# Position products of a two-layer attention kernel: all twelve heads at once, in one stage

## The reference

```python
# layer 0: attention over all 1024 positions, with relative positions
rel_h = jnp.einsum('bhwc,hkc->bhwk', r_q, Rh)
rel_w = jnp.einsum('bhwc,wkc->bhwk', r_q, Rw)
attn_bias = (rel_h[:, :, :, :, None] + rel_w[:, :, :, None, :]).reshape(Bx * NUM_HEADS, S, S)
scores = q @ jnp.swapaxes(k, -1, -2) * SCALE + attn_bias
out = softmax(scores) @ v
# layer 1: 7 x 7 neighbourhood attention plus 16 register tokens
scores = jnp.where(mask_cat[None, None], q @ k_cat.T * scale, NEG_INF)
```

## Time and profile before

| | |
|---|---|
| median of 3 runs | 4896.54 us (4892.41 to 4898.04) |
| the profiled execution | 4902.5 us, span 4900.8 us |
| TensorE matmul busy | 4491.2 us, 92% of the span |
| VectorE busy | 3079.3 us, 63% |
| ScalarE busy | 2608.5 us, 53% |
| POOL busy | 892.5 us, 18% |
| mean granted clock of TensorE | 0.951 |

### The profile page before, as it was taken

The page is one execution under the profiler, slowest core; times in us unless marked ns, Lnnn a source line. Parts: engine busy times, 40 slices in busy tenths (PEclk is TensorE's granted clock), DMA queues, the critical chain, the costliest instruction groups (busy, mean ns, idle before and its releaser), DMA issues.

```text
span 4900.8 us, 97559 instructions
## 1 busy us (share of the span) xinstructions
PE 4491.2 (92%) x32598; PEld 2291.5 (47%) x32598; DVE 3079.3 (63%) x5558; ACT 2608.5 (53%) x3955; POOL 892.5 (18%) x1901
## 2 busy tenths in 40 slices
PE   5879999999999999999999999999999999999998
PEld 3334453544535454453544535455454544535444
DVE  3736667665675656667566675656657566676654
ACT  1533556555564555556555564555646555565564
POOL 3112111222202212121212202212021121102111
PEclk7888999999999999999999999999999999999999
DMA  6334242443414433253433424433144432424401
GB/s 126 83 73 86 49 104 62 99 90 70 89 39 106 87 87 71 53 108 70 99 79 70 88 52 99 94 73 84 44 106 81 99 79 48 101 62 99 87 14 40
DMA packets 235869, 386.05 MB, mean 79 GB/s; under 512 B 58396, under 2 KB 133728, under 8 KB 235360
## 3 DMA queue, kind: packets, MB, share of 16 engines
q1 hardware_dynamic: 189280, 266.13, 23.8%
q10 hardware_dynamic: 21504, 75.51, 7.6%
q0 software_dynamic: 24576, 37.80, 4.8%
HBM read 227.79 MB, written 88.08 MB: 64 GB/s over the span
## 4 chain that ended last, share of the span: by engine, by line
PE 75%; DVE 9%; SPq 5%; issue 5%; DMA 5%; ACT 2%; DVEq 0%; ACTq 0%; POOL 0%
PE P L1135 15%; PE P L1153 14%; PE P L1094 13%; PE P L958 6%; PE P L959 6%; DVE mx L901 5%; PE P L1071 5%; PE P L1185 4%; PE P L1206 4%; PE P L1102 3%; DMA QA<-queries 2%; PE P L1178 1%; SPq L507 1%; DMA biases<-xn 1%; DVE mxc L907 1%
## 5 line engine op out<-in xcount | busy, mean ns | idle before, releaser
L901 DVE TENSOR_REDUCE mx<-P 128x1 f32<-128x512 f32 x3072 | 1923.2, 682 | 471.2 <-PE P L1094 467.9
L771 ACT ACTIVATE probs<-P 128x1024 f32<-128x1024 f32 x1536 | 1507.5, 1022 | 777.7 <-PE P L1153 777.0
L1094 PE MATMUL P<-K,AR 96*128 96x256 f16 x6144 | 1093.1, 282 | 42.9 <-DMA AR<-biases 26.7
L1153 PE MATMUL P<-AR,K 113*128 113x512 f16 x3072 | 924.8, 383 | 14.1 <-DMA AR<-mrow 13.6
L907 DVE TENSOR_REDUCE mxc<-P 128x1 f32<-128x336 f32 (+1 forms) x1536 | 648.2, 474 | 307.6 <-PE P L1103 304.0
L787 ACT ACTIVATE probs<-P 128x320 f32<-128x320 f32 (+3 forms) x1632 | 618.1, 436 | 405.2 <-PE P L1206 340.0
L1135 PE MATMUL P<-probs,V 128*17 128x512 f32 x6144 | 817.2, 604 | 9.9 <-ACT probs L771 9.9
L1094 PEld LDWEIGHTS P<-K,AR 96*128 96x128 f16 x6144 | 541.7, 99 | 566.9 <-DVE mx L901 198.3
L1153 PEld LDWEIGHTS P<-AR,K 113*128 113x128 f16 x3072 | 216.9, 98 | 676.6 <-ACT probs L771 517.8
L1206 PE MATMUL P<-A,K 113*128 113x320 f16 (+2 forms) x1536 | 447.1, 306 | 12.9 <-ACT probs L787 12.1
L1102 PE MATMUL P<-K,A 112*128 112x320 f16 (+1 forms) x1536 | 400.4, 295 | 53.4 <-DVE mx L901 35.8
(11 more groups left out here) (122 smaller groups left out, 3705.4 us busy)
## 6 DMA issues: line engine op xcount, KB each, us to landing
AR<-biases SPq DMA_DIRECT2D x384, 256.0 KB, 7.7
AR<-queries ACTq DMA_DIRECT2D x96, 512.0 KB, 5.8
biases<-xn SPq DMA_DIRECT2D x192, 256.0 KB, 2.9
AR<-queries ACTq DMA_DIRECT2D x96, 256.0 KB, 8.5
K<-oraw POOLq DMA_DIRECT2D x384, 64.0 KB, 4.8
xin<-in_x_dram SPq DMA_DIRECT2D x16, 768.0 KB, 10.5
queries<-oraw SPq DMA_DIRECT2D x384, 32.0 KB, 4.8
QA<-queries SPq DMA_DIRECT2D x192, 64.0 KB, 5.1
```

The lines of the kernel that those rows point to most:

```text
L771: nc.scalar.activation(probs[:, u % RING, j:j + 2, :], P[:, b:b + 2, :], ACT.Exp).then_inc(p_done[0], 1)
L901: V_.reduce_max(mx[:, n // 2, n % 2:n % 2 + 1], bank, AX.X).then_inc(used, 1)
L1094: last = mm(bank[:, QD * (v % 2):QD * (v % 2) + QD], AR[0:ROWS_MAX[0], part % SLOTS, v, c, j, 128 * q:128 * q + 128], K0[0:ROWS_MAX[0], h, ...
L1153: last = mm(P[:, j, :], K0[0:ROWS, h, 128 * kt:128 * kt + 128], AR[0:ROWS, p % SLOTS, kt // 2, :, j, :], start=True, stop=True)
```

## The change

The products of all 12 heads of image i+1 run in main1, in 16 jobs at steps 6 to 26 (`rel_jobs(image)`, `RELS = 16`). A job handles 2 lines, 2 matmuls each, of 192 columns, so a table's loaded operand serves all heads; `n // 8` is the table, and a bank holds 384 columns. QA holds all three groups and the first job waits for all of them. `relhi` and `rello` of the first table lie in `oraw`, those of the second in `xn` and in `xin`; ScalarE waits (`rel_moved`) for `biases_out` before its next output copy. Biases leave by table (2 x 3 stores), and the slots fill by table: at step 19 and at step 28. SP's `operands_out` now also issues the loads of QA of groups 1 and 2, that of group 1 ahead of group 2's stores, that of group 2 at the end. The first 22 maxima jobs of phase 1 stay in main1, the other 11 move to main0; the first 18 of local group 2 move from main1 to the main0 before it. POOL's row of ones is set once an image. `rcp` lies in QA's space.

```diff
-RELS = 4
+RELS = 16
+SECOND, THIRD = 22, 18
...
-    return {"rel": 4, "stat": 1, "max": (7, 5)[job[1]]}[job[0]]
+    return {"rel": 6, "stat": 1, "max": (7, 5)[job[1]]}[job[0]]
...
     else:
-        placed = evenly(max_jobs(0, image, 2), 0, 20)
+        placed = evenly(max_jobs(0, image, 1)[SECOND:], 0, 6) + evenly(max_jobs(0, image, 2), 6, 23)
...
-    placed += [(8 + n, job) for n, job in enumerate(rel_jobs(image, 2))]
...
-        placed += evenly(max_jobs(1, i1, 0), 13, 32) + evenly(max_jobs(1, i1, 1), 77, 94)
+        placed += evenly(max_jobs(1, i1, 0), 15, 34) + evenly(max_jobs(1, i1, 1), 75, 87)
+        placed += evenly(max_jobs(1, i1, 2)[:THIRD], 87, 95)
...
-    placed = evenly(max_jobs(1, image, 2), 0, 25)
-    placed += [(2 + n, job) for n, job in enumerate(rel_jobs(n0, 0))]
-    placed += [(0, ask(n0, 0)), (5, fill(n0, 0)), (6, ask(n0, 1)), (6, fill(n0, 1))]
-    placed += [(24 + n, job) for n, job in enumerate(rel_jobs(n0, 1))]
-    placed += [(28, ask(n0, 2)), (28, fill(n0, 2))]
-    placed += evenly(max_jobs(0, n0, 0) + max_jobs(0, n0, 1), 25, STEPS[1] - TAIL)
+    third = max_jobs(1, image, 2)[THIRD:]
...
+    rel = rel_jobs(n0)
+    placed = evenly(third[:8], 0, 6) + evenly(third[8:], 28, 38)
+    placed += evenly(rel, 6, 27) + [(0, ask(n0, 0)), (6, ask(n0, 1)), (28, ask(n0, 2))]
+    placed += [(19, fill(n0, p, 0)) for p in range(SLOTS)] + [(28, fill(n0, p, 1)) for p in range(SLOTS)]
+    placed += evenly(max_jobs(0, n0, 0) + max_jobs(0, n0, 1)[:SECOND], 39, STEPS[1] - TAIL)
...
+        QA = sb("QA", [128, G, GH, QD], F16)
+        staged = (flat[:, 0:G * S // 2], xn[:].rearrange("p a n -> p (a n)")[:, 0:G * S // 2])
+        relhi = [t.bitcast(F16).rearrange("p (m q) -> p m q", q=QD) for t in staged]
+        staged = (flat[:, G * S // 2:G * S], xin[:].rearrange("p t c -> p (t c)"))
+        rello = [t.bitcast(F16).rearrange("p (m q) -> p m q", q=QD) for t in staged]
...
-            def biases_away(im, g):
+            def biases_away(im, table):
...
-                    sp.wait_ge(ready, (im * G + g + 1) * RELS)
-                    for table in range(2):
+                    sp.wait_ge(ready, im * RELS + 8 * table + 8)
+                    for g in range(G):
...
-                    if g == 1:
-                        query_blocks(im, 0)
+                    if g:
+                        query_blocks(im, g - 1)
...
+                query_blocks(im, G - 1)
...
+            def rel_moved():
+
+                while staged_rel:
+                    image = staged_rel.pop()
+                    for table in range(2):
+                        act.wait_ge(biases_out[table], (image + 1) * PER_BIASES)
...
             def local_out(im, g, half):
 
                 rows_moved()
+                rel_moved()
...
-                    for b in range(8):
-                        line = 8 * (n % 2) + b
+                    for g in range(G if n == 0 else 0):
+                        pe.wait_ge(qa_in[g], (image + 1) * PER_QA)
+                    q = QA[:].rearrange("p g h (l w) -> p (g h) l w", w=16)
+                    table = n // 8
+                    for b in range(2):
+                        line = 2 * (n % 8) + b
                         rhs = q[:, :, :, line] if table else q[:, :, line, :]
                         for s in range(2):
                             lhs = Z[:, table, s, 15 - line:47 - line, :].rearrange("p x a -> p (x a)")
-                            last = mm(bank[:, 64 * b:64 * b + 64], lhs, rhs, start=(s == 0), stop=(s == 1))
+                            last = mm(bank[:, 16 * NH * b:16 * NH * b + 16 * NH], lhs, rhs,
+                                      start=(s == 0), stop=(s == 1))
```

More of the change, by code:

```diff
@@ L77, in max_jobs, with rel_jobs @@
     return [("max", layer, image, part, n) for n in range(ITEMS[layer] + 1)]
-def rel_jobs(image, g):
-    return [("rel", 0, image, g, n) for n in range(RELS)]
+def rel_jobs(image):
+    return [("rel", 0, image, 0, n) for n in range(RELS)]
 def stat_jobs(layer, image):
@@ L90, with fill, fills @@
 MOVES = ("fill", "ask")
-def fill(image, phase):
-    return "fill", 0, image, phase, 0
+def fill(image, phase, table):
+    return "fill", 0, image, phase, table
+def fills(image, phases):
+    return [fill(image, phase, table) for phase in phases for table in range(2)]
 def ask(image, phase):
@@ L198, in block_stages @@
     else:
-        yield "jobs", 0, n0, first_phases(n0, *max_jobs(0, n0, 1), *stat_jobs(1, i0))
+        yield "jobs", 0, n0, first_phases(n0, *max_jobs(0, n0, 1)[:0 if is_image(n0, 0) else SECOND], *stat_jobs(1, i0))
 def before_loop():
@@ L379, in consumed @@
             if kind == "rel":
-                return rello_done, (image * G + part) * RELS + n + 1
+                return rello_done, image * RELS + n + 1
             if kind == "stat":
@@ L486, in fill_slot @@
                     sp.wait_ge(st_done[0], im * STEPS[0] + (p - SLOTS + 1) * STEPS[0] // PHASES[0])
[L487 to L495, removed]
+                for b in range(2):
+                    rows_ = biases[g, table, D * b:D * b + D, :, 2 * half:2 * half + 2, :, :]
+                    rows_ = rows_.rearrange("k s a h n -> (k s) (a h n)")
+                    same = slice(2 * b, 2 * b + 2) if table == 0 else slice(b, VAR, 2)
+                    sp.dma_start(AR[32 * table:32 * table + 32, p % SLOTS, same, :, :, :],
+                                 rows_.unsqueeze(1).broadcast_to((32, 2, 2 * GH * QD))).then_inc(ar_in[p], 16)
@@ L514, in moves @@
                 if what == "fill":
-                    fill_slot(image, part)
-                    if part in (0, 2):
-                        query_blocks(image, part // 2 + 1)
-                    if part == 1 and is_image(image, 0):
+                    fill_slot(image, part, n)
+                    if part == SLOTS - 1 and n and is_image(image, 0):
                         static_rows()
-                if what == "rel" and n == RELS - 1:
-                    biases_away(image, part)
+                if what == "rel" and n % 8 == 7:
+                    biases_away(image, n // 8)
                 if what == "max" and n == ITEMS[layer]:
@@ L565, in stage @@
                         sp.wait_ge(mid_out, stored)
+                        if not (isinstance(im, int) and im + 2 >= B):
+                            sp.wait_ge(biases_out[1], (im + 3) * PER_BIASES)
                         sp.dma_start(xin[:], mid[im]).then_inc(mid_in, 16)
@@ L697, in stage @@
                 again = kind == "jobs" and any(job[0] == "rel" for e in after for _, job, _ in e)
-                if again or kind == "out" and (L == 0 or not (isinstance(im, int) and im + 2 >= B)):
-                    g, image = (1, im) if again else (2, im) if L == 0 else (1, im + 2)
-                    pool.wait_ge(biases_out[g], (image + 1) * PER_BIASES)
+                if again or kind == "out" and L == 1 and not (isinstance(im, int) and im + 2 >= B):
+                    image = im if again else im + 2
+                    pool.wait_ge(biases_out[1], (image + 1) * PER_BIASES)
                     take_wait()
-                    done, count = (ones_again, im + 1) if again else (ones_done[L], im + 1)
+                    done, count = (ones_again if again else ones_done), im + 1
                     nc.gpsimd.memset(xn[CH:CH + 1, 1, :], 1.0).then_inc(done, 1)
@@ L807, in high_parts @@
                     if job[0] == "rel":
+                        if job[4] == 0:
+                            rows_moved()
+                            staged_rel.append(job[2])
                         act.wait_ge(rel_done, consumed(job)[1])
@@ L1225, in deliver @@
                     last.then_inc(ot_done[L], 1)
-                if L == 0 or not (isinstance(im, int) and im + 2 >= B):
-                    pe.wait_ge(ones_done[L], im + 1)
+                if L == 1 and not (isinstance(im, int) and im + 2 >= B):
+                    pe.wait_ge(ones_done, im + 1)
                 for q in range(2):
```

56 lines of the change are left out of this document (27 added, 29 removed).

## The result

The changed kernel takes 5281.23 us (median of 4 runs, 5275.71 to 5288.34) against 4895.58 us before (4 runs): the ratio is 1.079, 95% interval 1.077 to 1.081. It is slower by 386 us. 258 us were forecast, with a range up to 5260, so the time lies just outside it. The profiled execution took 5277.37 us with a span of 5275.1, 374.3 us above that of before; the forecast for that difference was 257.

A forecast was written before the change was run, and what follows sets the result against it. TensorE, 75% of the span, was taken as the bound, with every wait ahead of it. Main1 +19.2 us and main0 -2.3 made +16.9 a turn, +237 over 14 turns, +257 with the ends: 5154 us, range 4950 to 5260.

The forecast's parts named there:

- The queries are needed earlier: Main1, step 6: TensorE waits for all three groups' queries, idle 17 us, going on at about +20.5.
- Steps 6 to 27: Main1 stretch holding the position products: 30 us, bounds 24 and 35, so step 28 begins at +50.5.
- price by the column: Second-table products in main1: every strided column costs 2.0 ns, so they still take 12.3 us.
- The new wait on ScalarE: Main1, behind step 29: first output copy waits for the biases; TensorE loses 6 us, bounds 0 and 8.
- about enough: Main1: second-table fills have ten steps until the maxima of phase 0 at step 39; no wait priced.
- Main1 as a whole: Sum of main1's terms: 101.5 us against 82.3, +19.2 a turn.
- Net -2.3 us: Main0: products leaving save 7.8 us, maxima jobs moved in add 5.5 with bank waits.
- covered while TensorE has more: Main0: VectorE's extra work of about 11 us on 111 of 151 was expected to cost no time.
- If the jobs no longer interleave so well, it is 0: Main0's unfavourable case: no net saving in place of -2.3 us.
- Ahead of the loop: Images 0 and 1 before the loop: later queries, more products and fills ahead of the maxima, +25 us together.
- The rivals: Main1: queries come in time, 4873 or 4790 us, chance 0.09; or little changes, 4895 us, chance 0.05.
- stride by matmul: Second-table products in main1: stride paid per matmul, 5.4 us in place of 12.3, total about 5000 us; chance 0.10.

The follow-up runs named there:

- ninth run: Changed kernel, query rows of slots 0 and 1 asked for at step 6 and of slot 2 at step 45 of main1: 5173.0 us.
- sixth run: Changed kernel, second table's products read adjacent columns as the first table's do (horizontal products left wrong): 5248.1 us.
- fourth run: Changed kernel, ScalarE's output copies wait for the biases of the first table alone: 5276.5 us.
- tenth: Changed kernel, 18 maxima jobs of local group 2 back in main1, 33 of local group 1 at main0 steps 77 to 94: 5226.0 us.
- thirteenth run: Changed kernel, moved maxima of phase 1 and local group 2 back in main1, local group 1's at main0 steps 77 to 94: 5253.9 us.

## Why the prediction was right in direction and too small

*The queries are needed earlier.* Right in mechanism and size. TensorE reached step 6 at +4.0 (forecast +3.5) and went on at +20.6 (+20.5). The ninth run shows the part of slot 0's fill, 4 us. The prediction did not say that fresh queries are not the only condition: without their wait, 6.6 us of waiting for ScalarE's copy space remain.

*Steps 6 to 27.* 25.3 us against a forecast of 30, near its lower bound: the first-table part went faster than taken, step 16 at +28.5. The second-table part took 17.4 us, forecast 20. The price by the column holds: a matmul of 192 columns takes 0.39 us (1.57 us for four), where a price by the matmul would have made 0.17. Four take 1.55 us at a granted clock of 1.00 (at 1624.57) and 1.57 at 0.50 (at 1630.62), and the sixth run with adjacent columns takes 7.0 us for the stretch. This agrees with the Trainium skill (SBUF — State Buffer, the note on cachelines): every strided column costs.

*The clock.* Main1 has 0.77 of its clock where it had 0.88. It falls twice ahead of step 28. The first fall, at 1604.0, lies within the long wait and lasts until 1621.1, in the first-table products. This agrees with the rule of the Trainium skill (TensorE: Matmul & The Clock Gate, Why this matters for your kernels) that spoke against the change. Then the full clock comes back, and goes again at 1627.9:

```profile
1621.10:1627.90 6.80, 6.80 (x56) 3.14 (x48) 3.49 (x7) 5.35 (x15) 0.00 (x0) 1.00 0.49 110
1627.90:1642.60 14.70, 14.70 (x77) 5.58 (x70) 3.91 (x7) 6.86 (x17) 0.00 (x0) 0.50 0.76 197
```

This second fall has no idle gap ahead of it: TensorE is busy throughout, with the strided products. With adjacent columns the sixth run keeps the full clock there. So the prediction was right to expect the low clock beside these products, and here the trace shows a fall that does not come from an idle gap.

*The new wait on ScalarE.* Right in place, too small: TensorE idled 7.36 us, and 4 were forecast with 2 for the clock. The fourth run shows that it hid an equal wait for the fills, which the prediction took as "about enough".

*Main1 as a whole*: +20.0 us, forecast +19.2. That it comes so near is in part luck, as errors cancelled: step 28 began at +45.9 and not at +50.5, and from there, wait included, it took 56.5 us where 6 + 45 were forecast.

*Main0* is the step that failed: "Net -2.3 us", measured +5.3, from 150.7 to 156.0. The terms as the runs give them: the products removed -6.8 (forecast -7.8); 11 jobs of phase 1 +3.6 (2.3); 18 of group 2 +2.6 (2.9); and two that the sum did not have, the shift of the maxima in steps 0 to 34, +2.5, and the squeeze of 33 maxima from 17 steps into 12, +3.7. Together +5.6; with 3.3 for the 11 jobs, as the tenth and thirteenth run give it, exactly +5.3. The prediction counted the jobs that came and went, at their back-to-back pace, and priced none that moved within the stage. VectorE did gain the 11 us that it named, but they were not "covered while TensorE has more": where two kinds of maxima stand in the same steps, TensorE waits for VectorE, as in steps 75 and 76. "If the jobs no longer interleave so well, it is 0" named the risk and bounded it at less than a third of its size. The 7.6 us in 14 turns are 106 of the 117 us that the profiled execution lies above its forecast; the medians, 128 us apart, hold 11 more of scatter between executions. Ahead of the loop it was +21 (forecast +25), at the end +1 (-5).

*The rivals* in which the time falls or stays did not come near; the stride by matmul is refuted.

## What to carry to other kernels

A wait at the end of a DMA chain has two levers, the order of the queue and what else is in the rings; here moving the wanted load forward in a strict queue displaced something that was wanted too and lost 50 us, while moving an unhurried fill out of its way cost one number and gave 1.3%. Before a gathering step (all heads at once) is moved to the earliest place, find when its last input lands, and put all independent work ahead of it. Price a job by how many stand in the same step, those of other kinds included, not by its back-to-back pace, and count the jobs that only change place.

## What the runs showed that had not been expected

- Crowding of jobs that share three banks: the same 33 maxima in 17 steps or in 12 differ by 3.7 us of the stage (0.11 us each). In the changed kernel VectorE is busy for only 23.7 of the 33.4 us of steps 75 to 95. That it is the three banks, and not the pace of VectorE alone, no run shows.
- A wait hides its successor: taking away 7.4 us of waiting on ScalarE gave 0.1 us a turn, since 7.96 us for a fill stood behind it; taking 10.4 us of strided matmuls away gave 2.2 us, since 8.2 of them came back as waiting.
- Stores of 256 KB that land in 2.4 to 2.6 us in quiet rings took up to 7.8 us with a fill of 768 KB issued beside them, and 10.6 to 11.2 us with the fills of a whole table just ahead as well (sixth run).
- The granted clock fell to half with TensorE busy 14.70 of 14.70 us, on strided moving columns; with adjacent columns, in the sixth run, it did not.
